# Latent stage: gate arithmetic and gated values on GpSimd, and identity products at other places of TensorE's queue

## The chip, the cores and the metric

The kernel runs on one core of a Trainium2 chip. A core has four compute engines with a queue of instructions each, TensorE (PE in the profile; the loading of its weights is PEld), VectorE (DVE), ScalarE (ACT) and GpSimd (POOL), and SyncE, which here only issues DMAs. Instructions of one engine start in the order in which they are written; between engines, and where a result is read back by the engine that wrote it, they wait on semaphores. Operands lie in SBUF (128 partitions; the profile names two large arenas WK and R) or in the eight PSUM banks ("bank"). The metric is the device time of one execution in microseconds; the kernel is compared by the median of several runs.

## The reference, cut to what matters

A tower of two layers over 32 x 128 tokens of width 192: embedding with a norm, quantised attention, a mixture of attention experts, the "latent" layer (a linear attention with gates, then a gated feed-forward part), and a last layer with attention and routed experts. The change is in the latent layer, of which these lines are computed for each group of tokens:

```
x_norm = rmsnorm(x, ln_w)
latent = silu(x_norm @ w_comp)
q, k, v = split(latent @ w_qkv, 3)
q_f = elu(rope(rmsnorm(q, qn_w))) + 1.0
k_f = elu(rope(rmsnorm(k, kn_w))) + 1.0
params = (latent @ w_reso).reshape(B, L, H, 4)
sem_amp, ctx_amp = sigmoid(params[..., 0]), sigmoid(params[..., 2])
sem_phase, ctx_phase = sigmoid(params[..., 1]) * pi, sigmoid(params[..., 3]) * pi
base_gate = sigmoid(sem_amp * ctx_amp * cos(sem_phase - ctx_phase) * temperature)
gate = clip(base_gate * 1.2 - 0.1, 0.05, 0.95)
kv_input = einsum('blhd,blhe->blhde', k_f, v) * gate[..., None, None]
...                        # decayed running sums over the tokens, times q_f, over their denominator
x = x + rmsnorm(out, memn_w) @ w_proj * silu(latent @ w_outgate)
x = x + silu(rmsnorm(x) @ w1) * (rmsnorm(x) @ w2) @ w3
```

The gate is one number for each token and head: 24 numbers for each partition in a step of the loop. The gated values are v times the gate, 384 numbers for each partition.

## The kernel before, in words

The work runs in stages one after the other: embedding and quantised attention (to about 447 us of the profile), expert attention (to 687), the latent stage (to 1167), the last layer's attention and routing (to 1604, here called the last attention), and the routed experts.

The latent stage treats 4096 tokens as 32 tiles of 128. Two streams of two tiles each (M = 2) take turns, NG = 8 times each, so that there are 16 steps. Each engine has its share of a step written as two generators, `*_l_1` (norm, latent, q, k, v, gates, scores and output) and `*_l_2` (projection, feed-forward part). `in_turns_apart` (L902, its loop L908) writes them out: `alternate(first(g, p1), second(g, p0))`, a piece of one, up to its `yield`, then a piece of the other. So while one stream is in its first half the other is in its second, and on every engine the order of the two is fixed by where the `yield`s stand. Nothing is reordered later.

What the change touches:

- `vector_l_1` (L1526). After the reduction of the squares (L1535) and nine small steps that build inverse roots (L1493 to L1501), VectorE rotates q and k (L1545 to L1549), takes the phase difference `a.z` of the gates (L1552), adds (L1553), scales and clamps each tile (L1556, L1558), forms the amplitude of the gate (L1559, L1560), builds the features (L1565) once ScalarE has the exponentials, forms the argument of the gate's tanh (L1568, L1569), copies half of the turned features out of PSUM (L1573), and multiplies scores by the decay table (L1588, four for each tile). Between the two tiles' L1588 it finishes the gate (L1578, L1579) and multiplies v by it (L1580), after which `f.value` is signalled. L1622 and L1626 belong to the other stream's second half.
- `scalar_l_1` (L1764). ScalarE takes the gates' tanh, silu and a copy of v out of PSUM (L1779 to L1781), then waits for `f.gate_in` and does the sine of `a.z` and its square (L1784, L1786), then the exponentials of the features (L1790, for which it loads another table), copies (L1794), and, when `f.gate_in` has come a second time, the tanh that is the gate (L1798).
- `pool_l_1`, `pool_l_2`. GpSimd only raises variances to the power -1/2 (L1047, called by `roots`).
- `tensor_l_1`, `tensor_l_2`: the product with w_comp (L1007), those with w_cat (L1701, L1704), the turning of the features (L1712), the scores (`products`, L1646), the values (`times_v`, L1656), and of the other stream the turning of the normalised rows (`turn_doubled`, L985 and L987), the hidden layer (L1674, L1682) and the last product (L1741).
- `stirred_f` (L1210) and `stirred` (L2037) are products of the identity with itself into a bank whose content isn't used; the expert attention calls the first, the last attention the second (`tensor_m_1`, L2042).
- The last attention's `tensor_m_1` waits for `f.x` (normalised rows from L1881), turns them, makes its features and scores (L2012), waits for the exponentials of the turned scores (`f.exp`, L2141 on ScalarE) and multiplies by v (L2025).

## Time and profile before

| | |
|---|---|
| median of 3 runs | 1988.45 us (1986.03 to 1989.02) |
| the profiled execution | 1987.9 us, of which the span of the profile is 1986.2 us |
| PE, PEld busy | 1551.4 us (78%), 1187.1 us (60%) |
| DVE busy | 1311.0 us (66%) |
| ACT busy | 959.7 us (48%) |
| POOL busy | 400.6 us (20%) |
| chain that ended last | PE 44%, DVE 37%, ACT 12%, issue 4% |

Busy shares are means over stages with different limits; in the latent stage POOL is busy for 43 of 480 us. The granted clock of TensorE has two levels here, 1.2 and 2.4 GHz, shown as 0.50 and 1.00; a stretch with a number between has parts at either. In a timeline, each row has start and duration in us, engine, line, operation, output and inputs with shapes, and in brackets how long the engine had been idle before it and who released it. A semaphore wait without idle time isn't shown.

### The profile page before, as it was taken

What the parts mean: (1) busy time and instruction counts of PE and PEld (TensorE: products, weight loads), DVE (VectorE), ACT (ScalarE), POOL (GpSimd) and SP (SyncE); (2) the same over time, 40 slices, a digit from 0 to 9 for tenths busy, and PEclk for the clock granted to TensorE, in tenths of its full rate; (3) what the DMA queues carried; (4) which work ended last, traced back from release to release, by engine and by line L of the source; (5) the groups of instructions that cost most, each with busy time, mean ns of one, the idle gap of its engine ahead of it and who ended that gap; (6) DMA issues with size and microseconds to landing.
All of it is one profiled execution on the core that took longest, in us unless ns stands there. A gap on an engine that the chain in (4) does not pass through costs nothing.

```text
span 1986.2 us, 36888 instructions
## 1 busy us (share of the span) xinstructions
PE 1551.4 (78%) x12764; PEld 1187.1 (60%) x12764; DVE 1311.0 (66%) x4361; ACT 959.7 (48%) x2769; POOL 400.6 (20%) x494
## 2 busy tenths in 40 slices
PE   0076764888888667887888868999999949999996
PEld 0032221776666445565555546777777738888885
DVE  7898885787888768878888844666666632222221
ACT  1275999863444544454454423444434324444442
POOL 7401332000000100000000000222222223333332
PEclk9985555569999779989999988999999959999998
DMA  3000000119990000000000000000000027778875
GB/s 75 17 1 1 1 1 1 22 42 185 180 164 5 1 0 1 0 0 0 0 0 0 0 24 3 26 25 24 24 24 24 25 88 181 193 199 192 194 192 141
DMA packets 136264, 113.02 MB, mean 57 GB/s; under 512 B 29417, under 2 KB 128457, under 8 KB 136137
## 3 DMA queue, kind: packets, MB, share of 16 engines
q1 hardware_dynamic: 119320, 91.70, 20.2%
q0 software_dynamic: 16864, 20.33, 5.3%
q8 instruction: 42, 0.69, 0.1%
q14 instruction: 38, 0.30, 0.1%
HBM read 69.19 MB, written 45.94 MB: 58 GB/s over the span
## 4 chain that ended last, share of the span: by engine, by line
PE 44%; DVE 37%; ACT 12%; issue 4%; POOL 1%; DVEq 0%; DMA 0%; ACTq 0%; POOLq 0%; SPq 0%
ACT bank L716 9%; PE bank L2357 8%; PE bank L2347 6%; PE bank L1007 5%; PE bank L2342 3%; PE bank L1000 3%; PE bank L2012 3%; DVE R L1588 2%; DVE WK L1588 2%; DVE R L1864 2%; PE bank L2025 1%; PE bank L2040 1%; PE bank L1712 1%; PE bank L966 1%; PE bank L640 1%
## 5 line engine op out<-in xcount | busy, mean ns | idle before, releaser
L1047 POOL TENSOR_TENSOR WK<-WK,mhalf 128x2 f32<-128x2 f32 (+1 forms) x96 | 78.0, 812 | 806.9 <-DVE WK L1512 324.5
L2394 ACT ACTIVATE R<-bank,R 128x256 f32<-128x256 f32 x234 | 98.2, 471 | 187.3 <-PE bank L2347 185.5
L716 ACT ACTIVATE bank<-bank,nbias,sc 128x128 f32<-128x128 f32 x384 | 168.9, 993 | 21.3 <-POOL nbias L528 21.3
L2274 POOL DMA_INDIRECT moe_sum<-WK x78 | 121.5, 1557 | 229.0 <-DMA moe_sum<-WK 165.3
L2245 DVE SCALAR_TENSOR_TENSOR WK<-bank,R,WK 128x192 f32<-128x192 f32 x78 | 28.9, 413 | 209.4 <-PE bank L2357 209.4
L716 ACT ACTIVATION_READ_ACCUMULATOR bank<-bank,nbias,sc 128x1 f32 x384 | 163.2, 768 | 0.0
L2357 PE MATMUL bank<-R 128*128 128x192 f32 x936 | 158.6, 326 | 0.0
L1007 PE MATMUL bank<-WK,R 96*128 96x256 f32 x576 | 148.3, 400 | 6.5 <-ACT WK L973 3.8
L2357 PEld LDWEIGHTS bank<-R 128*128 128x128 f32 x936 | 151.3, 190 | 0.0
L1007 PEld LDWEIGHTS bank<-WK,R 96*128 96x128 f32 x576 | 106.9, 195 | 26.2 <-ACT WK L973 6.9
L2347 PE MATMUL bank<-R 128*128 128x256 f32 x468 | 112.8, 392 | 0.0
L610 PE MATMUL bank<-R 32*128 32x128 bf16 x384 | 62.9, 300 | 59.9 <-ACT bank L716 57.1
L2347 PEld LDWEIGHTS bank<-R 128*128 128x128 f32 x468 | 86.8, 192 | 23.6 <-issue 13.2
L610 PEld LDWEIGHTS bank<-R 32*128 32x128 bf16 x384 | 29.6, 118 | 118.7 <-ACT bank L716 106.6
L433 DVE TENSOR_REDUCE neg_all<-bank 128x3 f32<-128x384 f32 x128 | 69.5, 554 | 27.3 <-PE bank L610 25.1
L2012 PE MATMUL bank<-WK 32*128 32x128 f32 x1536 | 63.5, 296 | 24.5 <-ACT R L2141 12.4
L559 PE MATMUL bank<-R,wq 96*128 96x512 bf16 x192 | 79.0, 540 | 4.6 <-DVE WK L407 2.7
L1674 PE MATMUL bank<-WK,R 128*128 128x256 f32 x256 | 68.1, 412 | 15.0 <-ACT WK L993 15.0
L1000 PE MATMUL bank<-R,WK 96*128 96x192 f32 x384 | 76.4, 343 | 2.9 <-ACT WK L973 1.4
L528 POOL TENSOR_SCALAR nbias<-neg_all,sc 128x3 f32<-128x3 f32 x128 | 38.6, 301 | 198.1 <-DVE neg_all L433 197.8
L2040 PE MATMUL bank<-ident 128*128 128x128 f32 x480 | 76.6, 299 | 0.0
L315 PE MATMUL bank<-ident,amx 128*1 128x128 f32 (+2 forms) x5 | 1.9, 382 | 93.8 <-DVE amx L351 54.9
(499 smaller groups left out, 3996.9 us busy)
## 6 DMA issues: line engine op xcount, KB each, us to landing
moe_rows_in<-zeros SPq DMA_DIRECT2D x1, 25026.0 KB, 148.2
R<-in_L_ffn_w SPq DMA_DIRECT2D x39, 576.0 KB, 5.0
R<-in_L_ffn_w SPq DMA_DIRECT2D x39, 384.0 KB, 3.1
R<-moe_rows_in SPq DMA_DIRECT2D x39, 194.0 KB, 4.6
R<-in_L_ffn_w SPq DMA_DIRECT2D x78, 96.0 KB, 3.6
R<-in_L_ffn_b SPq DMA_DIRECT2D x39, 96.0 KB, 5.1
moe_sum<-resid POOLq DMA_DIRECT2D x16, 192.0 KB
moe_sum<-WK POOLq DMA_INDIRECT x78, 5.8
```

Source lines behind the costliest of these rows:

```text
L559: mm = nc.tensor.matmul(bank[b][:, :], wq[0:C, c, o * P:(o + 1) * P], tokens(xqT_all, g)[0:C, c, :], start=(c == 0), stop=(c == 1))
L610: mm = nc.tensor.matmul(bank[u % 4][:, k * P:(k + 1) * P], qk[32 * j:32 * j + 32, k, i * P:(i + 1) * P], qk[32 * j:32 * j + 32, 3 + k, i * ...
L716: ins = nc.scalar.activation(s, s, ACT.Exp, bias=nbias[:, u, k:k + 1], scale=col(SS), accum_out=units(sum_all, g, u)[:, k:k + 1])
L1000: mm = nc.tensor.matmul(a.bank[b][:, i * D:(i + 1) * D], a.xT[0:C, c, i * P:(i + 1) * P], w[0:C, c, :], start=(c == 0), stop=(c == 1))
L1007: mm = nc.tensor.matmul(out, w[0:C, c, m], a.xT[0:C, c, :], start=(c == 0), stop=(c == 1))
L1588: nc.vector.tensor_tensor(a.p[:, 4 * i + j, :], a.bank[j][:, 0:384], decay[:, j, :], ALU.mult).then_inc(f.decayed, 1)
L2012: mm = nc.tensor.matmul(a.bank[j][:, k * P:(k + 1) * P], x, y, start=True, stop=True)
L2040: nc.tensor.matmul(a.bank[1][:, 0:P], ident[:, :], ident[:, :], start=True, stop=True)
L2274: pool.indirect_dma_start(out=acc, out_offset=bass.IndirectOffsetOnAxis(ap=x_id[k % B3][:, t:t + 1].bitcast(U32), axis=0), in_=x_y[k % B3] ...
L2347: mm = nc.tensor.matmul(hidden_at(p, n), xw_1a[h][:, q * P:(q + 1) * P], x_T[h][:, 0, :], start=False, stop=True)
L2357: mm = nc.tensor.matmul(bank[7][:, t * D:(t + 1) * D], x_hid[f][:, t * P:(t + 1) * P], xw_2[h][:, f, :], start=(p == 0 and n == 0 and t == ...
L2394: ins = nc.scalar.activation(x_hid[q], hidden_at(p, n), ACT.Gelu, bias=xb_1[h][:, q:q + 1])
```

## The change

Twelve instructions on GpSimd take the place of eight on VectorE (seven on 24 columns and the multiplication L1580), in another form: 1/8 is put into the amplitude, 1 - 2 s^2 is written as amplitude - 2 amplitude s^2, the temperature is applied by ScalarE's tanh (`scale=l_temp`), the constants 0.6 and 0.5 come from a small tile `l_gc` that is filled once, and one instruction on a single column (L1642 of the changed kernel) stands ahead of the clamp. GpSimd waits on a new semaphore `f.gate_w` for its own results. `f.gate_in` now comes three times a step. Two identity products are added ahead of the products with w_cat, five ahead of the turning for the feed-forward part; in the last attention two at the start of `tensor_m_1` go, and the two behind the second tile's turned scores become five ahead of the wait for the first tile's exponentials. Left out of the diff are the counts of semaphores, the two new names in `l_signals` and `take(3)` for `l_gc`.

```diff
...
@@ -1453,7 +1453,8 @@
-            yield
+            for n, x in enumerate((0.6, 0.5, 1.0)):
+                nc.gpsimd.memset(l_gc[:, n:n + 1], x)
             for a in streams:
...
@@ -1462,6 +1463,8 @@
             ins.then_inc(s_pad, 1)
+            pool.wait_ge(s_pad, 4)
+            yield
...
@@ -1548,37 +1551,23 @@
             ch.step(ins)
-            v.wait_ge(f.gates, per(g, 1, 1))
-            nc.vector.tensor_tensor(a.z, a.sg[:, :, :, 1], a.sg[:, :, :, 3], ALU.subtract).then_inc(f.gate_in, 1)
             ch.step(nc.vector.tensor_tensor(a.qk, a.a, a.b, ALU.add))
...
                 nc.vector.tensor_scalar(a.b[:, w], a.a[:, w], 0.0, None, ALU.min).then_inc(f.features_in, 1)
-            ch.step(nc.vector.tensor_scalar(a.pz, a.sg[:, :, :, 2], 1.0, None, ALU.add))
-            ch.step(nc.vector.scalar_tensor_tensor(out=a.amp, in0=a.sg[:, :, :, 0], scalar=1.0, in1=a.pz, op0=ALU.add,
-                                                   op1=ALU.mult))
             for i in range(M):
...
                                                in1=heads(a.qk[:, w]), op0=ALU.max, op1=ALU.add).then_inc(f.pads, 1)
-            v.wait_ge(f.gate_t, per(g, 2, 1))
-            ch.step(nc.vector.tensor_scalar(a.pz, a.z2, -2.0, 1.0, ALU.mult, ALU.add))
-            nc.vector.scalar_tensor_tensor(out=a.pz, in0=a.pz, scalar=l_temp, in1=a.amp, op0=ALU.mult,
-                                           op1=ALU.mult).then_inc(f.gate_in, 1)
             for i in range(M):
...
             decayed(v, g, a, f, 0)
-            v.wait_ge(f.gate_t, per(g, 2, 2))
-            ch.step(nc.vector.tensor_scalar(a.z, a.z, 0.6, 0.5, ALU.mult, ALU.add))
-            ch.step(nc.vector.tensor_scalar(a.z, a.z, 0.05, 0.95, ALU.max, ALU.min))
-            nc.vector.tensor_tensor(a.va[:, :, :, 0:DH], a.r.rearrange("p t (h d) -> p t h d", d=DH),
-                                    a.z.unsqueeze(3).to_broadcast([P, M, H, DH]), ALU.mult).then_inc(f.value, 1)
             decayed(v, g, a, f, 1)
...
@@ -1625,9 +1614,36 @@
+        def of_gate(n):
+
+            return l_gc[:, n:n + 1].to_broadcast([P, M * H]).rearrange("p (t h) -> p t h", t=M)
+
         def pool_l_1(pool, g, a, f):
...
             yield
+            pool.wait_ge(f.gates, per(g, 1, 1))
+            nc.gpsimd.tensor_tensor(a.z, a.sg[:, :, :, 1], a.sg[:, :, :, 3], ALU.subtract).then_inc(f.gate_in, 1)
+            nc.gpsimd.tensor_scalar(a.pz, a.sg[:, :, :, 2], 1.0, None, ALU.add)
+            nc.gpsimd.tensor_scalar(a.amp, a.sg[:, :, :, 0], 0.125, 0.125, ALU.mult, ALU.add).then_inc(f.gate_w, 1)
+            pool.wait_ge(f.gate_w, per(g, 6, 1))
+            nc.gpsimd.tensor_tensor(a.amp, a.amp, a.pz, ALU.mult).then_inc(f.gate_w, 1)
+            pool.wait_ge(f.gate_w, per(g, 6, 2))
+            nc.gpsimd.tensor_tensor(a.pz, a.amp, a.amp, ALU.add).then_inc(f.gate_w, 1)
+            pool.wait_ge(f.gate_w, per(g, 6, 3))
+            pool.wait_ge(f.gate_t, per(g, 2, 1))
+            nc.gpsimd.tensor_tensor(a.pz, a.pz, a.z2, ALU.mult).then_inc(f.gate_w, 1)
+            pool.wait_ge(f.gate_w, per(g, 6, 4))
+            nc.gpsimd.tensor_tensor(a.pz, a.amp, a.pz, ALU.subtract).then_inc(f.gate_in, 1)
+            pool.wait_ge(f.gate_t, per(g, 2, 2))
+            nc.gpsimd.tensor_tensor(a.z, a.z, of_gate(0), ALU.mult).then_inc(f.gate_w, 1)
+            pool.wait_ge(f.gate_w, per(g, 6, 5))
+            nc.gpsimd.tensor_tensor(a.z, a.z, of_gate(1), ALU.add).then_inc(f.gate_w, 1)
+            pool.wait_ge(f.gate_w, per(g, 6, 6))
+            nc.gpsimd.tensor_tensor(a.pz[:, 0, 0:1], l_gc[:, 2:3], l_gc[:, 2:3], ALU.mult)
+            nc.gpsimd.tensor_scalar(a.z, a.z, 0.05, 0.95, ALU.max, ALU.min).then_inc(f.gate_in, 1)
+            pool.wait_ge(f.gate_in, per(g, 3, 3))
+            nc.gpsimd.tensor_tensor(a.va[:, :, :, 0:DH], a.r.rearrange("p t (h d) -> p t h d", d=DH),
+                                    a.z.unsqueeze(3).to_broadcast([P, M, H, DH]), ALU.mult).then_inc(f.value, 1)
...
@@ -1696,6 +1712,7 @@
             product(a, lw_comp, slice(0, LAT), a.bank[1][:, 0:NM]).then_inc(f.lat_p, 1)
+            stirred_f(a, 2)
             pe.wait_ge(f.lat, per(g, 1, 1))
...
@@ -1727,6 +1744,7 @@
             yield
+            stirred_f(a, 5)
             pe.wait_ge(f.ffn_in, per(g, 1, 1))
...
@@ -1780,7 +1798,7 @@
             ins.then_inc(f.gates, 1)
-            act.wait_ge(f.gate_in, per(g, 2, 1))
+            act.wait_ge(f.gate_in, per(g, 3, 1))
             nc.scalar.activation(a.z2, a.z, ACT.Sin, scale=float(np.pi / 4)).then_inc(f.gate_s, 1)
...
@@ -1794,8 +1812,8 @@
             yield
-            act.wait_ge(f.gate_in, per(g, 2, 2))
-            nc.scalar.activation(a.z, a.pz, ACT.Tanh, scale=0.125).then_inc(f.gate_t, 1)
+            act.wait_ge(f.gate_in, per(g, 3, 2))
+            nc.scalar.activation(a.z, a.pz, ACT.Tanh, scale=l_temp).then_inc(f.gate_t, 1)
             for i in range(M):
...
@@ -2040,7 +2058,6 @@
         def tensor_m_1(pe, g, a, f, prev):
-            stirred(a, 2)
             pe.wait_ge(f.x, per(g, 1, 1))
...
@@ -2072,9 +2089,9 @@
             yield
+            stirred(streams[1 - a.n], 5)
             pe.wait_ge(f.exp, per(g, 4 * M, 4))
             scores(pe, g, a, f, 1, f.scoresT, True)
-            stirred(streams[1 - a.n], 2)
             pe.wait_ge(f.exp, per(g, 4 * M, 5))
```

On POOL, at the start of the latent stage, the first root and the fills of the padded tiles were followed by the loop:

```order
L1047 TENSOR_TENSOR WK<-WK,mhalf 128x4
L1458 MEMSET WK 128x1536
L1459 MEMSET R 128x768
L1458 MEMSET R 128x1536
L1459 MEMSET R 128x768
L1463 MEMSET R 128x24 x2
L908 UNCONDITIONAL_BRANCH
L908 ISA
```

Now, behind the last of the same fills and ahead of the loop, the first step's gate stands there with its twelve instructions:

```order
L1625 TENSOR_TENSOR WK<-WK 128x24
L1626 TENSOR_SCALAR WK<-WK 128x24
L1627 TENSOR_SCALAR WK<-WK 128x24
L1629 TENSOR_TENSOR WK<-WK 128x24
L1631 TENSOR_TENSOR WK<-WK 128x24
L1634 TENSOR_TENSOR WK<-WK 128x24
L1636 TENSOR_TENSOR WK<-WK 128x24
L1638 TENSOR_TENSOR WK<-WK 128x24
L1640 TENSOR_TENSOR WK<-WK 128x24
L1642 TENSOR_TENSOR WK<-WK 128x1
L1643 TENSOR_SCALAR WK<-WK 128x24
L1645 TENSOR_TENSOR R<-WK 128x24x16
```

In the loop the same twelve stand behind the other stream's two roots (L1047 128x2) and ahead of the next step's root (L1047 128x4).

On DVE, in the loop, a step from the second part of the rotation (L1549) to the copies out of PSUM was:

```order
L1549 TENSOR_TENSOR R<-R 128x2x192 x2
L1552 TENSOR_TENSOR R<-WK 128x24
L1553 TENSOR_TENSOR R<-R 128x768
L1556 TENSOR_TENSOR R<-R,WK 128x384
L1558 TENSOR_SCALAR R<-R 128x384
L1556 TENSOR_TENSOR R<-R,WK 128x384
L1558 TENSOR_SCALAR R<-R 128x384
L1559 TENSOR_SCALAR R<-WK 128x24
L1560 SCALAR_TENSOR_TENSOR WK<-WK,R 128x24
L1565 SCALAR_TENSOR_TENSOR R<-R 128x24x16 x2
L1568 TENSOR_SCALAR R<-R 128x24
L1569 SCALAR_TENSOR_TENSOR R<-R,WK 128x24
```

The same place in the changed kernel, whose lines are numbered otherwise from here on (L1552 is L1549 of before, L1554 is L1553, L1557 and L1559 are L1556 and L1558, L1563 is L1565):

```order
L1552 TENSOR_TENSOR R<-R 128x2x192 x2
L1554 TENSOR_TENSOR R<-R 128x768
L1557 TENSOR_TENSOR R<-R,WK 128x384
L1559 TENSOR_SCALAR R<-R 128x384
L1557 TENSOR_TENSOR R<-R,WK 128x384
L1559 TENSOR_SCALAR R<-R 128x384
L1563 SCALAR_TENSOR_TENSOR R<-R 128x24x16 x2
L1567 COPY R<-bank 128x384 x2
```

Five small instructions are gone here (L1552, L1559, L1560, L1568, L1569). The other two (L1578, L1579) and the large multiplication L1580 stood between the two groups of four L1588; they now follow each other, as L1577 x8.

On PE, a step of the latent stage from the product with w_comp to the turning for the feed-forward part was, and is now:

```order
L1007 MATMUL bank<-WK,R 128x256 x2
L1701 MATMUL bank<-R 128x384 x2
L1704 MATMUL bank<-R 128x432 x2
L985 MATMUL bank<-ident,WK 128x128
L987 MATMUL bank<-ident,WK 64x128 x2
```

```order
L1007 MATMUL bank<-WK,R 128x256 x2
L1213 MATMUL bank<-ident 128x128 x2
L1718 MATMUL bank<-R 128x384 x2
L1721 MATMUL bank<-R 128x432 x2
L1213 MATMUL bank<-ident 128x128 x5
L985 MATMUL bank<-ident,WK 128x128
L987 MATMUL bank<-ident,WK 64x128 x2
```

Two products (L1213) stand behind L1007 and five ahead of L985. Next, PE in the last attention, from the router's product of one stream to the product with v of the other, before and after:

```order
L2100 MATMUL bank<-R,WK 128x8 x4
L2012 MATMUL bank<-WK 128x128 x12
L2040 MATMUL bank<-ident 128x128 x2
L2025 MATMUL bank<-R 32x128 x12
L2040 MATMUL bank<-ident 128x128 x2
L2044 REGISTER_ALU
L966 MATMUL bank<-ident,WK 96x128 x4
L2025 MATMUL bank<-R 32x128 x12
```

```order
L2117 MATMUL bank<-R,WK 128x8 x4
L2058 MATMUL bank<-ident 128x128 x5
L2030 MATMUL bank<-WK 128x128 x12
L2043 MATMUL bank<-R 32x128 x12
L2061 REGISTER_ALU
L966 MATMUL bank<-ident,WK 96x128 x4
L2043 MATMUL bank<-R 32x128 x12
```

Here L2040 (L2058 in the changed kernel) are the identity products, L2100 (L2117) the router's product, L2012 (L2030) the turned scores, L2025 (L2043) the product with v and L966 the turning of the next rows.

## Rows read from the trace of the kernel before

**Rows 1.** One stretch of the span, the latent stage (start:end, its length, busy us and count of each engine, granted clock, DMA share, GB/s).

```profile
687.00:1167.00 480.00, 372.12 (x3144) 266.54 (x3143) 384.69 (x1192) 230.80 (x638) 42.86 (x54) 0.94 0.00 0
```

**Rows 2.** The same view by steps of the latent stage.

```profile
841.57:873.00 31.43, 26.59 (x184) 18.85 (x180) 23.65 (x74) 14.01 (x40) 2.46 (x3) 0.84 0.00 0
...
902.14:930.23 28.09, 22.31 (x186) 15.84 (x180) 23.63 (x74) 13.93 (x40) 2.46 (x3) 1.00 0.00 0
```

**Rows 3.** The timeline of one step of the latent stage.

```profile
915.33 0.38 ACT L1781 ACTIVATE R<-bank 128x192 f32<-128x192 f32 x1
...
917.35 0.20 DVE L1552 TENSOR_TENSOR R<-WK 128x24 f32<-128x24 f32 x1
...
917.47 0.95 DVE L1553 TENSOR_TENSOR R<-R 128x768 f32<-128x768 f32 x1
...
917.58 0.22 ACT L1784 ACTIVATE R<-R 128x24 f32<-128x24 f32 x1 [1.87 <-DVE R L1552]
...
918.08 1.28 ACT L1790 ACT_TABLE_LOAD   x1
...
919.05 0.36 DVE L1558 TENSOR_SCALAR R<-R 128x384 f32<-128x384 f32 x1
...
920.30 0.52 ACT L1790 ACTIVATE R<-R 128x384 f32<-128x384 f32 x1 [0.34 <-DVE R L1558]
...
923.62 0.95 PE L1646 MATMUL bank<-R 32*128 32x128 f32 x24 [0.85 <-ACT R L1794]
```

**Rows 4.** The same timeline, later in the step.

```profile
927.66 1.95 DVE L1588 TENSOR_TENSOR R<-bank,decay 128x384 f32<-128x384 f32 x4 [0.18 <-PE bank L1646]
...
929.66 1.52 PE L1656 MATMUL bank<-R 128*32 128x128 f32 x48 [0.57 <-DVE R L1588]
```

**Rows 5.** The same timeline, TensorE.

```profile
909.20 1.56 PE L1701 MATMUL bank<-R 128*128 128x384 f32 x4 [0.47 <-ACT R L1768]
...
912.42 0.33 PE L985 MATMUL bank<-ident,WK 128*128 128x128 f32 x1 [0.21 <-DVE WK L1616]
...
914.68 2.00 PE L1674 MATMUL bank<-WK,R 128*128 128x256 f32 x8 [0.94 <-ACT WK L993]
...
921.24 1.53 PE L1712 MATMUL bank<-ident,R 128*128 128x128 f32 x12 [0.70 <-DVE R L1565]
```

**Rows 6.** The timeline where POOL and DVE use SBUF together, two earlier stages.

```profile
38.26 0.19 POOL L2495 TENSOR_TENSOR shift<-less_mean,rs 128x4 f32<-128x4 f32 x1
...
50.43 0.96 DVE L221 SCALAR_TENSOR_TENSOR WK<-resid,pos 128x768 f32<-128x768 f32 x1
...
50.76 0.69 POOL L2495 TENSOR_TENSOR shift<-less_mean,rs 128x4 f32<-128x4 f32 x1
...
203.34 0.99 POOL L523 TENSOR_TENSOR resid<-resid,bprojb 128x384 f32<-128x384 f32 x1
...
203.74 0.88 DVE L422 TENSOR_SCALAR R<-WK 128x512 bf16<-128x512 f32 x1
...
206.38 0.43 DVE L422 TENSOR_SCALAR R<-WK 128x512 bf16<-128x512 f32 x1
```

**Rows 7.** The timeline, five identity products of the expert attention.

```profile
448.30 1.38 PE L1213 MATMUL bank<-ident 128*128 128x128 f32 x10 [1.14 <-DVE amx L1314]
```

**Rows 8.** The stretches view by steps of the last attention.

```profile
1214.06:1242.27 28.21, 25.15 (x270) 21.54 (x270) 12.56 (x40) 11.51 (x27) 1.70 (x2) 0.87 0.01 1
...
1267.91:1291.76 23.85, 21.88 (x249) 18.55 (x248) 16.50 (x65) 9.68 (x25) 6.65 (x8) 1.00 0.08 27
...
1291.76:1316.36 24.60, 22.99 (x262) 19.51 (x266) 16.53 (x66) 10.85 (x27) 6.63 (x8) 1.00 0.08 26
...
1340.22:1366.20 25.98, 24.38 (x251) 20.67 (x252) 16.54 (x66) 10.36 (x25) 6.63 (x8) 0.90 0.07 23
```

**Rows 9.** The timeline in the last attention.

```profile
1318.37 0.64 PE L966 MATMUL bank<-ident,WK 128*96 128x128 f32 x4 [0.72 <-DVE WK L1881]
...
1339.20 0.95 PE L2012 MATMUL bank<-WK 32*128 32x128 f32 x24 [0.71 <-ACT R L2141]
```

8 lines of the change are left out of this document (4 added, 4 removed).

## Prediction

> **What bounds the kernel now.** I read the stretches of the span first, then the latent stage step by step, then the timeline of one step, then the places where POOL and DVE already meet, and last the steps of the last attention. The latent stage takes 480 of 1986 us; DVE is busy for 385 of them, PE for 372, and POOL, which gets the new work, for only 43 [rows 1]. So there is room on POOL, but a mean says nothing about which wait ends last. That is read from one undisturbed step [rows 3 to 5]; the sixteen steps repeat it.
>
> The rows of DVE from the rotation to the clamps carry no idle time in brackets: it works there without a gap, and the phase difference L1552 and the sum L1553 lie in that run [rows 3]. ScalarE waits 1.87 us for L1552, does sine and square, loads a table from 918.08 to 919.36, and has it just before the first clamped tile L1558 is there at 919.41 (start 919.05 and 0.36 of duration). The second exponential starts at 920.30 behind the second L1558 with 0.34 us idle. From there the chain is ScalarE's: exponential, another table, two silus, two copies, and then the scores L1646 at 923.62, which waited for its copy. So DVE is on the path up to 920.3 and not between there and the scores. Between the two groups of four L1588 PE makes the second tile's scores, and DVE waits 0.18 us for them although L1578 to L1580 stand in that place [rows 4]: these three instructions lie in PE's shadow. L1656, which needs the gated values, starts at 929.66, released by the last L1588.
>
> **The change part by part.** The sum is made against the profiled execution's 1987.9 us; the median of the runs shown is 0.55 us above it.
>
> VectorE's work that goes. L1559, L1560, L1568 and L1569 stand behind 920.3, where ScalarE's chain is later, and L1578 to L1580 stand in PE's shadow; I cost them at nothing, and no new wait shows up, because the next things due (ScalarE's copy at 923.62, PE's scores at 927.66) don't depend on them. L1552 is on the path: L1553 starts 0.12 us behind it (917.35 to 917.47), so a step gets 0.12 us shorter. 16 x 0.12 = 1.9 us. Below that no gain, above it none.
>
> GpSimd's chain. The gates' values are there when L1781 ends, 915.71. If a POOL instruction on 24 columns takes 0.2 to 0.7 us, which are the free and the blocked time of one on 4 columns [rows 6], the phase difference is there at 916.0 to 916.5, earlier than DVE's 917.55; even 0.8 us later (the five products, below) it still is in time. ScalarE's wait for it has until 917.58 before the table load becomes late. The last five instructions follow ScalarE's tanh, which stands just behind the copy that released L1646 at 923.62, so at about 924.2: four at 0.2 to 0.7 and a product of 384 columns, 0.99 us for the same shape at L523 [rows 6], give 926.0 to 928.0, and PE needs them at 929.66. Behind the gate in POOL's queue stands the root of the next step, which starts at 930.23 [rows 2], so nothing is late there. Cost 0 in the middle; the far end is a rival.
>
> The Trainium skill, page "GPSIMD Engine Reference", section "4.1 Engine selection", says to keep elementwise work on VectorE since GpSimd is about twice as slow with two inputs. The trace agrees (0.99 us at L523 against 1.95 us for the four L1588, 0.49 us each, all of 384 columns, is its ratio), and by that rule the move would lose; by the row the loss falls into a wait of 1.7 us or more, and the sum doesn't change.
>
> Both engines on SBUF at once. In the changed kernel seven POOL instructions of the gate run beside DVE's unbroken run. Earlier stages show what happens: a POOL product of 0.19 us took 0.69 where DVE's L221, with two inputs in SBUF, was running; L221 itself kept its 0.96. The other way round, L422 on DVE started while POOL's L523 was running and took 0.88 instead of 0.43, to the end of L523 [rows 6]. So whoever comes second waits for the first. A POOL instruction of about 0.2 to 0.3 us that gets in between two of DVE's holds the second for at most its own length. The lower end is 0 a step; the upper end is one collision as long as the one seen, 0.45 a step, 7.2 us. I take 0.1 a step, near the lower end, because the POOL instructions are a fifth as long as L523: 1.6 us.
>
> The Trainium skill, page "SBUF — State Buffer", section "🔬 SBUF: two separate sides", calls it an exclusive lock on a shared pair of ports, taken for a whole instruction, and names DVE's instructions with two SBUF inputs too. The trace agrees for POOL waiting on L221; by that rule each of the seven could stop DVE, and the sum would be worse by up to 16 x 7 x 0.2 = 22 us, an estimate with the 0.19 us of the row.
>
> Three fills of one column each stand in the first step ahead of the large ones, for which DVE and PE wait: bounded by 0 and 3 x 0.19, taken as 0.2 us.
>
> Identity products. Five, shown as ten entries, take 1.38 us [rows 7], so two about 0.55. The two behind L1007 fall into a wait of 0.47 us and PE has its silu'd input at 909.20 [rows 5]: with the overlap of successive products they just fit, 0 to 0.1 us. The five stand ahead of L985, where PE waited only 0.21 us [rows 5]. L985 gets about 0.8 us later, with it the hidden layer (L1674 waits 0.94 for ScalarE's copy, and that wait moves along), which ended at or before 920.5 and now ends by about 921.3; the turning L1712 waited 0.70 us there. So nearly all of it is absorbed, and what is left is behind ScalarE's table anyway. In the last attention, L966 waits 0.72 us behind the two products that go, and the five that come stand in a wait of 0.71 us and delay the second turned scores by about 0.4 to 0.6 us [rows 9]; L966, behind them, waits for DVE and not for them. I cost the direct time of all at 0.
>
> What they can give back is the clock. An undisturbed step of the latent stage takes 28.09 us at a granted clock of 1.00; the step at 841.57 took 31.43 with 0.84 [rows 2], 3.3 us more. Of ten such rows two others are below 1.00 behind the stage's cold start and add 0.8. In the last attention steps alternate between 24.60 and 23.85 us. The step from 1214.06 took 28.21 with 0.87 and the one from 1340.22 took 25.98 with 0.90, 4.4 and 1.4 us more [rows 8]; of fourteen such rows five others lie below 1.00 and add 4.6. Together 4.1 + 10.4 = 14.5 us are lost to stretches in which half the clock, 1.2 GHz, was granted. The drops follow PE's light stretches: in the latent stage the small turnings L985 with waits on either side, in the last attention the router's product and the wait at 1339.20. The five products stand just there. But in the latent stage the light stretch behind them (L985 to L1674) stays as long as it was, and two products elsewhere go. Ends: all 14.5 us back, or two more drops like 31.43's, 6.6 us lost. I take a third back: 4.9 us.
>
> Sum: 1987.9 - 1.9 + 1.6 + 0.2 - 4.9 = 1982.9 us profiled, 1983.5 as a median.
>
> **Rivals.**
>
> The clock isn't helped. The drops come at other steps, as many as before. Then 1987.8 profiled, 1988.3 us. For it: the latent stage has undisturbed steps with exactly the same gaps as the disturbed one, so the gaps alone don't decide. Against: the products fill the emptiest place.
>
> The drops all go: 1987.8 - 14.5, so 1973.8 us. For it: the expert attention already has such products in its waits [rows 7], and its steps show few drops. Against: the long wait ahead of L966 and L1000 is left as it is.
>
> POOL's first subtraction comes late (slower). If it misses its gap between the L1549 and waits for L1553 (0.95 us from 917.47, so to 918.42), the phase difference ends at about 918.7, the sine starts 1.15 us later than 917.58, and table, exponentials and all of ScalarE's chain follow, because the table load had 0.05 us to spare. 16 x 1.15 = 18.4 us instead of the 1.6: 1999.7 profiled, 2000.2 us. It decides from a phase difference later than 917.6 on. For it: L2495 waited out a whole L221. Against: the gates are there at 915.71 and the phase difference is wanted at 917.58, with two seams between DVE's instructions before that.
>
> PE becomes late. If the five products delay the hidden layer by more than L1712's wait of 0.70 us, by up to 0.5 a step, 8 us come on top, 1987.8 + 8 - 4.9 and so 1991.4 us. For it: 1.38 less 0.21 is more than 0.70. Against: successive products overlap, and ScalarE's table load hides some.
>
> **How the numbers follow.** A measurement of this kernel tells 0.2%, 4.0 us, from no change. My forecast (clock partly helped) has 37%, the clock not helped 25%, all drops gone 15%, POOL late 12%, PE late 11%. Faster by over 0.2%, under 1984.5: 30 of the 37, all of the 15, 2 of the 25, 0.47. Slower, over 1992.4: all 12, 5 of the 11, 3 of the 25, 0.20. The rest 0.33. The range reaches down past the case without drops, 1973.8, to 1972 (no cost of the shared SBUF at all), and up past PE's late case, a third of the way to POOL's late chain, to 1995; the longer way to 2000 is left out.
>
> **What would show it.** Right: L1784 starts before 917.6 in the same step's time and the first exponential still waits for DVE; the undisturbed steps take 28.0 and 29.0 us; POOL's product ends more than 1 us ahead of L1656; fewer steps below a clock of 1.00. Wrong: the exponential's table load ends behind L1558, L1553 and L1558 on DVE are longer than 0.95 and 0.36 us, L1712 has no wait left, or as many steps below 1.00 as before.

## The result: faster by 18 us, more than forecast, and the profile after

The changed kernel takes 1970.09 us in the median of five runs (1966.6 to 1974.8) against 1988.64 us (1986.03 to 1989.07); the ratio is 0.991, interval 0.9894 to 0.9925. The forecast was 1983.5 with a range from 1972 to 1995, so the direction was right and the time lies 2 us below the range. The profiled execution took 1969.73 us, its span is 1968.1 us. Two executions of this study ran in a slower state and stand in no time or ratio given here: one of the kernel before, of 4086.57 us, beside e8 to e11, and one of e13, of 2076.66 us.

Split at the same instructions of both traces, the spans differ like this:

| stretch | before | after | difference |
|---|---|---|---|
| up to the first step of the latent stage | 687.19 | 685.94 | -1.25 |
| fifteen steps of the latent stage | 444.10 | 436.87 | -7.23 |
| its last half step, opening of the last attention | 58.14 | 59.26 | +1.12 |
| fifteen steps of the last attention | 374.14 | 364.44 | -9.70 |
| the rest | 422.62 | 421.59 | -1.03 |

The two loops hold nearly all of it. The first row lies ahead of anything that was changed (over all traces of this study the latent stage begins between 683.3 and 689.5 us). The stretches view of the kernel after, the latent stage and two of its steps, then three steps of the last attention (columns as in rows 1):

```profile
687.00:1167.00 480.00, 389.10 (x3380) 296.12 (x3381) 364.18 (x1063) 233.41 (x643) 124.37 (x249) 0.95 0.00 0
838.58:866.60 28.02, 23.41 (x198) 17.70 (x194) 22.30 (x66) 14.01 (x40) 7.62 (x15) 1.00 0.00 0
866.60:895.50 28.90, 24.67 (x246) 18.95 (x242) 22.44 (x67) 14.55 (x40) 7.59 (x15) 1.00 0.00 0
1206.87:1232.02 25.15, 23.20 (x274) 19.89 (x276) 12.56 (x40) 11.41 (x27) 1.71 (x2) 1.00 0.01 1
1328.55:1353.14 24.59, 22.54 (x268) 19.16 (x260) 16.52 (x67) 10.41 (x25) 6.65 (x8) 1.00 0.07 24
1353.14:1376.98 23.84, 21.80 (x248) 18.81 (x252) 16.48 (x65) 9.79 (x24) 6.64 (x8) 1.00 0.07 25
```

Here every step behind the first of each loop is at a granted clock of 1.00, but for the second of the latent stage (0.94), which still holds the end of the cold start. The two first steps have 0.55 and 0.78, as before the change (0.55 and 0.77). Against [rows 8] the steps of the last attention are as long as the undisturbed ones of before (24.60 and 23.85), so nothing was gained there but the drops: 28.21 became 25.15, and 25.98 became 24.59. In the latent stage two things came together: no drop, and shorter steps, 28.02 against 28.09 us [rows 2], and 28.90 against 29.15 for the long ones.

The timeline of one step of the latent stage after the change:

```profile
908.72 1.99 PE L1690 MATMUL bank<-WK,R 128*128 128x256 f32 x8 [0.94 <-ACT WK L993]
...
909.83 0.45 POOL L1625 TENSOR_TENSOR R<-WK 128x24 f32<-128x24 f32 x1 [5.30 <-ACT R L1799]
...
910.31 0.22 ACT L1802 ACTIVATE R<-R 128x24 f32<-128x24 f32 x1 [0.56 <-POOL R L1625]
...
910.72 0.96 DVE L1554 TENSOR_TENSOR R<-R 128x768 f32<-128x768 f32 x1
...
910.82 0.95 POOL L1627 TENSOR_SCALAR WK<-WK 128x24 f32<-128x24 f32 x1
...
912.70 0.52 ACT L1808 ACTIVATE R<-R 128x384 f32<-128x384 f32 x1 [0.62 <-DVE R L1559]
...
913.48 1.23 DVE L1563 SCALAR_TENSOR_TENSOR R<-R 128x384 f32<-128x384 f32 x2
...
913.59 0.52 ACT L1808 ACTIVATE R<-R 128x384 f32<-128x384 f32 x1 [0.37 <-DVE R L1559]
...
914.40 1.47 PE L1729 MATMUL bank<-ident,R 128*128 128x128 f32 x12
...
915.26 1.21 DVE L1567 COPY R<-bank 128x384 f32<-128x384 f32 x2 [0.55 <-PE bank L1729]
...
918.93 0.84 POOL L1645 TENSOR_TENSOR R<-R 128x384 f32<-128x384 f32 x1
...
920.95 1.95 DVE L1577 TENSOR_TENSOR R<-bank,decay 128x384 f32<-128x384 f32 x4 [1.07 <-PE bank L1662]
```

POOL's phase difference is there at 910.28, 0.44 us before VectorE even begins the sum L1554; the rival of a late POOL chain did not come. ScalarE has its table 0.62 us ahead of the first clamped tile, where it had 0.05 us to spare before [rows 3], so VectorE's run alone sets when the exponentials start. The gated values end at 919.77, 3.2 us ahead of the product that needs them. The turning L1729 has no wait left (0.70 before, [rows 5]): the five products took up just the room that was read there. The prediction had named this as a sign of being wrong, and it came; what it was to show, longer steps, didn't. VectorE's copies behind it now wait for it, some 0.55 us, but ScalarE, which has the table load to do, doesn't, and the step got no longer. And POOL does collide with VectorE, but it is POOL that pays: L1627, on 24 columns, takes 0.95 us, as long as the L1554 that it stands beside. L1554 itself takes 0.96 against 0.95 before [rows 3].

### The profile page after: what moved, and what is told of

Read it like the earlier page. It is cut to its first block, busy times and chain, and to the rows that moved or that the text cites. A ratio compares the mean times of both kernels' runs of the same rounds, so it can differ in the third digit from the quotient of the medians.

```text
span 1968.1 us, 37567 instructions
## 1 busy us (share of the span) xinstructions
PE 1551.7 (79%) x13020; PEld 1205.5 (61%) x13020; DVE 1289.9 (66%) x4233; ACT 961.6 (49%) x2769; POOL 481.7 (24%) x689
## 4 chain that ended last, share of the span: by engine, by line
PE 46%; DVE 34%; ACT 12%; issue 4%; POOL 2%; DVEq 0%; DMA 0%; ACTq 0%; POOLq 0%; SPq 0%
ACT bank L716 9%; PE bank L2374 8%; PE bank L2364 6%; PE bank L1007 5%; PE bank L2359 3%; PE bank L1000 3%; PE bank L2030 2%; PE bank L1690 2%; DVE R L1577 2%; DVE WK L1577 2%; DVE R L1882 2%; PE bank L966 1%; PE bank L640 1%; PE bank L641 1%; PE bank L1718 1%
## 5 line engine op out<-in xcount | busy, mean ns | idle before, releaser
L1047 POOL TENSOR_TENSOR WK<-WK,mhalf 128x2 f32<-128x2 f32 (+1 forms) x96 | 78.7, 819 | 546.0 <-DVE WK L1024 247.1
L1007 PE MATMUL bank<-WK,R 96*128 96x256 f32 x576 | 147.5, 398 | 6.2 <-ACT WK L973 3.5
L1007 PEld LDWEIGHTS bank<-WK,R 96*128 96x128 f32 x576 | 106.2, 194 | 25.9 <-ACT WK L973 6.6
L2140 ACT ACTIVATE WK<-bank,R 128x256 f32<-128x256 f32 x96 | 40.3, 471 | 69.4 <-PE bank L1007 69.4
L966 PE MATMUL bank<-ident,WK 128*96 128x128 f32 x320 | 53.0, 290 | 26.1 <-DVE WK L1899 11.6
```

The source lines that it names most:

```text
L1007: mm = nc.tensor.matmul(out, w[0:C, c, m], a.xT[0:C, c, :], start=(c == 0), stop=(c == 1))
L1047: nc.gpsimd.tensor_tensor(a.rs[:, 0:n], a.ve[:, 0:n], mhalf[:, 0:n], ALU.pow).then_inc(f.root, 1)
```

## Experiments

The kernel before, run many times beside these, gave anything from 1977.8 to 1992.1 us in one set; the fastest of these runs had a mean granted clock of 0.887, the slowest 0.877. So the same program loses more or less to low-clock stretches from run to run. A "drop" is such a stretch inside a step. The verdicts below rest on medians, and on steps of the traces, which don't depend on how many drops a run had.

### One part of the change at a time

e1 puts the identity products back (only the gate is changed). The other three leave the gate on VectorE: e2 has only the products of the latent stage, e3 only those of the last attention, e4 both. Edits against the kernel before, cut at "...":

```diff
 e2, e4:    product(a, lw_comp, ...).then_inc(f.lat_p, 1)
+           stirred_f(a, 2)
 ...
 e2, e4:    yield
+           stirred_f(a, 5)
            pe.wait_ge(f.ffn_in, per(g, 1, 1))
 ...
 e3, e4: def tensor_m_1(pe, g, a, f, prev):
-           stirred(a, 2)
 ...
 e3, e4:    yield
+           stirred(streams[1 - a.n], 5)
            pe.wait_ge(f.exp, per(g, 4 * M, 4))
            scores(pe, g, a, f, 1, f.scoresT, True)
-           stirred(streams[1 - a.n], 2)
```

> The change with the identity products put back where they were in both stages: only the gate on GpSimd is left. Theory (products keep the clock up, the gate is worth little): the undisturbed steps of the latent stage become 0.06 us (short ones) to 0.25 us (long ones) shorter, some 2.5 us in all, the steps of lower clock stay, as many as before in both stages (14.5 us), and the median is 1986 us (1984 to 1989). Rival 1 (the gate's move brought much of the gain, because VectorE's chain is shorter): under 1980. Rival 2 (where drops fall is a matter of how the steps happen to lie in time, and any edit moves them): the drops are at other steps, and their sum may be anything between 0 and 14.5 us.

> The kernel before with the two and the five identity products of the latent stage, nothing else. Theory (each stage's products keep that stage's clock): no step of the latent stage below a clock of 1.00 behind the cold start, the last attention as before (25.6 to 28.2 us at its disturbed steps), a gain of 4 us and so 1984.5 us (1982 to 1987). Rival 1 (gate): no gain, 1988.6, or a loss of up to 5 us, since the five products delay the hidden layer by 0.7 us while DVE isn't relieved. Rival 2 (alignment): the drops move in both stages, and the last attention changes too although nothing of it is changed.

> The kernel before with the changed products of the last attention only (two at the start of its step gone, two moved and made five). Theory: no step of the last attention below 1.00 but its cold start, the latent stage as before; about 10 us gained, 1978.5 us (1976 to 1982). Rival 1 (gate): no gain. Rival 2 (alignment): part of the drops stay, at other steps, 1980 to 1988.

> All identity products as in the change, the gate still on VectorE. Theory: no drops in both stages, 14.5 us gained, 1974 us (1971 to 1977), so that the changed kernel's 1970.1 is this and some 3 to 4 us of the gate. Rival 1 (gate): above 1980. Rival 2 (alignment): drops left in one of the stages.

| | median, us | ratio to before, interval | undisturbed latent steps | latent steps with a drop | low-clock stretches in the last attention |
|---|---|---|---|---|---|
| e1 gate | 1987.53 | 0.9997 (0.9983 to 1.0011) | 28.10, 28.98 | 4 | 8 |
| e2 latent products | 1987.46 | 0.9999 (0.9985 to 1.0013) | 28.07, 29.14 | 2 | 6 |
| e3 last attention | 1981.62 | 0.9973 (0.9958 to 0.9988) | 28.08, 29.14 | 6 | 0 |
| e4 e2 and e3 | 1976.39 | 0.9949 (0.9929 to 0.9969) | 28.07, 29.15 | 3 | 0 |

Before had 3 such latent steps and 8 such stretches. The last attention is settled: with its products moved, not one drop; without, 6 and 8. The gate and the latent products alone are worth nothing in the median, where some 2.5 and 4 us were expected: their traces still have drops, e1 even a step of 31.36 us, and e2's two contradict its expectation of none. e3 and e4 lie in their ranges, but above the times named, and e4 has three drops where none was expected. Compared with each other, e4 is 5.2 us below e3: on top of the last attention's products those of the latent stage are worth something, with the gate still on VectorE. The undisturbed steps say who shortened them: the products hardly (28.07, 29.14), the gate by 0.17 us in the long ones. The stretches of e3's last attention, at the place of a drop before:

```profile
1337.76:1362.35 24.59, 22.56 (x268) 19.19 (x260) 16.53 (x66) 10.38 (x25) 6.63 (x8) 1.00 0.07 24
1362.35:1386.19 23.84, 21.79 (x247) 18.80 (x250) 16.48 (x65) 9.80 (x24) 6.62 (x8) 1.00 0.07 25
```

### The changed kernel again, and with one part out

e5 is the changed kernel once more; e6 leaves out the two and the five products of the latent stage, e7 the two only. Edits against the changed kernel, cut at "...":

```diff
 e6, e7
-            stirred_f(a, 2)
             pe.wait_ge(f.lat, per(g, 1, 1))
 ...
 e6
-            stirred_f(a, 5)
             pe.wait_ge(f.ffn_in, per(g, 1, 1))
```

> The changed kernel, nothing left out, once more. What is open: whether the latent stage is free of drops because products and gate together remove their cause, or by chance in the one profile, as the steps happened to lie in time. Theory (cause removed): again every step behind the stage's first two at 1.00, 28.0 and 28.9 us, and 1970 us (1966 to 1975). Rival (chance): one to four steps of the latent stage below 1.00, each 0.6 to 3.3 us longer, and a median nearer to 1975.

> The changed kernel without the two and five products of the latent stage: gate on GpSimd, and the changed products of the last attention. The last attention is free of drops in any theory. Theory (the latent products are needed too): four or so steps of the latent stage below 1.00, as where the gate alone was moved, 8 us, and 1979 us (1976 to 1984). Rival (the gate's shorter steps do it, the latent products are worth nothing, as they were by themselves): no more drops than in the changed kernel and the same time within 2 us, 1970 to 1972.

> The changed kernel without the two products behind L1007, the five ahead of L985 kept. Theory (the five do it, since the light stretch begins at L985): like the changed kernel, 1970 us (1966 to 1975), no drops in the latent stage. Rival (the two count as much, since each wait that is filled counts): one to three steps below 1.00 and 1973 to 1978.

e5 took 1971.45 us (1966.93 to 1976.82, ratio 0.9931, 0.9911 to 0.9951), and one of its latent steps has a drop (29.70 us). So "no drop" in the first profile was partly luck. e6 took 1977.76 (0.9953, 0.9937 to 0.9969), with two drops: added to gate and last attention, the latent products are worth some 6 us, much as without the gate (e4 against e3), though alone they showed nothing. The intervals of these neighbours overlap, so the 5 to 6 us are rough. They also shorten the undisturbed steps once the gate is on POOL: e6 has 28.10 and 28.97, like e1, against 28.02 and 28.90; the five do this, since e7 has 28.03 and 28.90. e7 took 1972.77 us in the median (0.9952, 0.9916 to 0.9987), but its runs fall into two groups: seven from 1967.1 to 1975.3 us and three from 1992.8 to 1994.6, above every run of the changed kernel (at most 1976.8 in twelve). So the two are not idle either, against its expectation. The profiled run is one of the three, 1992.8 us, and the most telling trace of all: five short steps at a clock of 0.84 to 0.89, four of them the same. The stretches view of e7, one such step and its three parts:

```profile
901.07:933.60 32.53, 27.70 (x198) 20.11 (x191) 22.13 (x65) 14.16 (x40) 6.55 (x15) 0.84 0.00 0
901.07:905.24 4.17, 2.65 (x30) 1.51 (x19) 3.21 (x15) 2.31 (x9) 1.62 (x2) 1.00 0.00 0
905.24:915.48 10.24, 9.74 (x20) 6.48 (x21) 4.89 (x15) 3.60 (x12) 0.87 (x2) 0.50 0.00 0
```

And the kernel before, its slow step of [rows 2] and the start of that of [rows 8], cut in the same way:

```profile
841.57:845.77 4.20, 2.65 (x27) 1.51 (x19) 3.21 (x15) 2.33 (x9) 1.67 (x2) 1.00 0.00 0
845.77:856.01 10.24, 9.77 (x20) 6.40 (x21) 4.98 (x16) 3.52 (x11) 0.79 (x2) 0.50 0.00 0
856.01:873.00 16.99, 14.18 (x139) 10.93 (x141) 15.46 (x44) 8.16 (x21) 0.00 (x0) 1.00 0.00 0
1340.22:1340.70 0.48, 0.48 (x4) 0.38 (x4) 0.16 (x1) 0.48 (x2) 0.23 (x1) 1.00 0.00 0
1340.70:1344.12 3.42, 3.42 (x33) 2.62 (x32) 1.81 (x5) 1.75 (x6) 0.77 (x1) 0.50 0.00 0
```

The clock falls 4.2 us into the step in both, ahead of the five products and even of the two (6.4 us in). It falls behind a stretch in which PE worked 2.65 of 4.2 us. Over all traces of latent stages up to here, each drop of a short step begins 3.5 to 4.9 us into it. So the latent products stand behind the place where this clock is lost. The two stand inside the drop, though, and there they seem to matter: in all traces of this study no drop of a short step lasts over 6.9 us in a kernel that has them (ten drops), and without them eight of nineteen last 10.2 or 10.3 us. That is a count and no tested cause.

Two of before's three drops are of another kind. They begin 13.5 us into a long step, and there the prediction had the place right. The stretches view of before and its timeline:

```profile
811.82:825.30 13.48, 10.57 (x83) 6.69 (x76) 9.61 (x38) 7.48 (x25) 2.46 (x3) 1.00 0.00 0
825.30:828.71 3.41, 3.41 (x11) 2.32 (x11) 3.25 (x9) 1.40 (x6) 0.00 (x0) 0.50 0.00 0
...
824.73 3.27 PE L1674 MATMUL bank<-WK,R 128*128 128x256 f32 x8 [0.94 <-ACT WK L993]
```

This fall comes 0.6 us behind the end of the light stretch from L985 to L1674, ahead of which the five now stand. None of the kernels with the five has a drop of this kind (e2 and e4 with the gate on VectorE among them), and none with the gate on POOL and without the five has one either (e1, e6 and, below, e10). In before both together cost 1.2 us, against 3.3 us for the one in the short step.

In the last attention the drop of before begins at 1340.70, 1.5 us behind the end of the wait of 0.71 us of [rows 9], and the five moved products stand exactly in that wait. From this came the next set.

### Place against number

Four products in the wait of 1.33 us that ends 2.8 us into a step, behind the turning back: e8 adds them to the changed kernel, e9 has only them and the last attention's change, e10 has them in place of the two and five. e11 takes the last attention's numbers but leaves the place of before. e8 and e10 are edits of the changed kernel, e9 and e11 of the kernel before:

```diff
 e8, e9, e10
             turned_back(pe, g, a, f, 1)
+            for _ in range(4):
+                nc.tensor.matmul(a.bank[1][:, 0:P], ident[:, :], ident[:, :], start=True, stop=True)
             pe.wait_ge(f.out, per(g, M, M))
 ...
 e11
         def tensor_m_1(pe, g, a, f, prev):
-            stirred(a, 2)
 ...
             scores(pe, g, a, f, 1, f.scoresT, True)
-            stirred(streams[1 - a.n], 2)
+            stirred(streams[1 - a.n], 5)
```

> The changed kernel with four more identity products in each latent step, behind the turning back (L1680) and ahead of the wait for the output's rows (L966). In all profiles so far the latent stage's low-clock stretches begin 3.5 to 4.9 us behind the start of a short step, so ahead of the two and the five products of the change, and right behind this wait of 1.33 us. Theory (a drop is prevented by products ahead of where it begins, those behind only shorten it): no drop in the latent stage, and 1969 us (1965 to 1973), a little under the changed kernel's 1970 to 1971. Rival (place doesn't matter, only how many): also none, so this run tells nothing of the two by itself. Rival (four products delay L966): each step 0.1 to 0.3 us longer, 1973.

> The kernel before with the last attention's changed products and, in the latent stage, only the four ahead of L966: no two, no five, gate on VectorE. Theory (the place decides): no drops at 3.5 to 4.9 us into a step, undisturbed steps of 28.1 and 29.15 us, and 1973 us (1970 to 1976), better than 1976.4 with the two and five in their places. Rival (the gate's move is what makes the drops rarer): two to five drops left, 1978 to 1983.

> The changed kernel with the four ahead of L966 in place of the two and the five of the latent stage. Theory (place): no drops that begin 3.5 to 4.9 us into a step, 1970 us (1967 to 1974). Rival (the two and five are needed, since they end a drop early and shorten the long steps by 0.1 us): 1975 to 1979.

> The kernel before with the last attention's products changed in number but not in place: the two at the step's start gone, and five instead of two behind the second tile's turned scores (as written before the change), none ahead of them. The latent stage as before. Theory (place): the drops of the last attention stay, three to five pairs of 1.4 to 2 us, and 1986 us (1982 to 1990). Rival (number): no drops there, as with the change's place, and 1981 us.

e11 took 1988.54 us (0.9999, 0.9986 to 1.0013) and kept its drops in the last attention; a pair of its steps, by the stretches view:

```profile
1344.62:1370.71 26.09, 24.49 (x253) 20.78 (x254) 16.53 (x66) 10.28 (x25) 6.64 (x8) 0.90 0.07 23
1370.71:1395.36 24.65, 23.05 (x253) 19.91 (x254) 16.48 (x65) 10.10 (x24) 6.64 (x8) 0.96 0.07 24
```

Where the five stand, by the timelines of the changed kernel and of e11:

```profile
1326.68 1.36 PE L2058 MATMUL bank<-ident 128*128 128x128 f32 x10
1327.97 0.95 PE L2030 MATMUL bank<-WK 32*128 32x128 f32 x24
...
1343.63 0.95 PE L2012 MATMUL bank<-WK 32*128 32x128 f32 x24 [0.71 <-ACT R L2140]
1344.51 1.92 PE L2040 MATMUL bank<-ident 128*128 128x128 f32 x10
```

In e11 they come some 1.7 us later, counted from the router's product, the wait of 0.71 us ahead of L2012 stays empty, and they do nothing: there the place decides. Its trace has eight drops in this stage, as before's has.

In the latent stage e8 took 1970.37 us (0.9906, 0.9881 to 0.9932), e9 1974.45 (0.9931, 0.9904 to 0.9958), e10 1972.02 (0.9918, 0.9892 to 0.9945), with four runs each, all as expected, like e11's. None of their traces has a drop at 3.5 to 4.9 us of a short step. The pairs that differ by the four alone show the gain: e9 lies 7.2 us below e3, and their intervals only touch, at 0.9958; e10 lies 5.7 us below e6, with overlapping intervals. e9, in which the gate stays on VectorE and the five are absent, has two drops of the other kind: 13.5 us into one long step and 13.6 us into the last full one. This kind stands in before, e3, e9 and e11 alone, the kernels that have neither the gate on POOL nor the five ahead of L985. That is read from sixteen traces and is not a tested cause. The price of the four is nothing, by the wait in the changed kernel and by e8's timeline:

```profile
898.32 0.64 PE L966 MATMUL bank<-ident,R 128*96 128x128 f32 x4 [1.33 <-DVE R L1588]
...
900.42 1.06 PE L1741 MATMUL bank<-ident 128*128 128x128 f32 x8
901.91 0.64 PE L966 MATMUL bank<-ident,R 128*96 128x128 f32 x4 [0.43 <-DVE R L1588]
```

Of the 1.33 us of waiting 0.43 are left, and e8's undisturbed steps are 28.01 and 28.89 us. In the medians, though, e8 isn't below the changed kernel.

### What of the gate shortens the steps, and the starts of stages

e12 puts the phase difference back on VectorE, e13 the gated values, both against the changed kernel. In e12 the addition of 1 on POOL (`a.pz`) also became an instruction with two inputs. e14 is e8 with products once at the starts and ends of stages. Cut at "...":

```diff
 e12
-            nc.gpsimd.tensor_tensor(a.z, a.sg[:, :, :, 1], a.sg[:, :, :, 3], ALU.subtract).then_inc(f.gate_in, 1)
+            v.wait_ge(f.gates, per(g, 1, 1))
+            nc.vector.tensor_tensor(a.z, a.sg[:, :, :, 1], a.sg[:, :, :, 3], ALU.subtract).then_inc(f.gate_in, 1)
             ch.step(nc.vector.tensor_tensor(a.qk, a.a, a.b, ALU.add))
 ...
-            nc.gpsimd.tensor_scalar(a.pz, a.sg[:, :, :, 2], 1.0, None, ALU.add)
+            nc.gpsimd.tensor_tensor(a.pz, a.sg[:, :, :, 2], of_gate(2), ALU.add)
 e13
             decayed(v, g, a, f, 0)
+            v.wait_ge(f.gate_in, per(g, 3, 3))
+            nc.vector.tensor_tensor(a.va[:, :, :, 0:DH], ..., ALU.mult).then_inc(f.value, 1)
             decayed(v, g, a, f, 1)
 ...
-            pool.wait_ge(f.gate_in, per(g, 3, 3))
-            nc.gpsimd.tensor_tensor(a.va[:, :, :, 0:DH], ..., ALU.mult).then_inc(f.value, 1)
 e14 (against e8)
 tensor_l_1:
+            if isinstance(g, int) and g == 0:
+                stirred_f(a, 13)
 ...
             pe.wait_ge(f.gates, per(g, 1, 1))
+            if isinstance(g, int) and g == 0:
+                stirred_f(a, 16)
 ...
 tensor_l_2:
-            stirred_f(a, 5)
+            stirred_f(a, 14 if isinstance(g, int) and a.n else 5)
 ...
 tensor_m_1:
+            if not prev and not a.n:
+                stirred(streams[1 - a.n], 10)
```

> The changed kernel with the phase difference back on VectorE, behind the rotation, the rest of the gate on GpSimd. Theory (the gate's gain per step is this one instruction leaving VectorE's unbroken run): undisturbed steps become 0.12 us longer than 28.02 and 28.90, so 28.14 and 29.02 us, 2 us in all, lost in the spread of the medians (1970 to 1976). Rival (the gain of the long steps, 0.25 us, is from somewhere else, or the shared SBUF costs something that goes away with it): steps unchanged within 0.03 us, or shorter.

> The changed kernel with the gated values multiplied on VectorE between the two tiles' decay products, as before the change; the gate itself stays on GpSimd. Theory (that instruction stood in TensorE's shadow): undisturbed steps as in the changed kernel, 28.02 and 28.90 us within 0.03, and the wait of DVE for the second tile's scores falls from 1.07 us to about 0.5. Rival (it was on the path, or its POOL form costs DVE time): steps 0.2 us or more longer or shorter.

> The changed kernel with the four products ahead of L966 and, once each, products in the long waits where stages begin and end at the low clock: 13 ahead of the first rows of the latent stage (a wait of 6.33 us), 16 ahead of the first turning of features (8.05 us), 14 in place of 5 in the stage's last step (2.86 us), 10 ahead of the first rows of the last attention (4.93 us). Theory (products ahead of a stretch bring the clock up for it): the first latent step falls from 35.6 to some 33 us, the one behind it from 31.2 to 30 us, the step that opens the last attention from 25.1 to 24 us, and the time to 1965 us (1960 to 1969). Rival (a single burst in a wait doesn't hold the clock until the work arrives): 1970 us as with the four alone.

The stretches view, a long and a short undisturbed step of e12, then of e13:

```profile
812.64:841.80 29.16, 24.67 (x246) 18.88 (x238) 22.57 (x68) 14.57 (x40) 6.96 (x14) 1.00 0.00 0
841.80:869.96 28.16, 23.42 (x202) 17.70 (x198) 22.41 (x67) 13.99 (x40) 7.37 (x14) 1.00 0.00 0
```

```profile
810.29:839.18 28.89, 24.66 (x248) 18.94 (x238) 22.89 (x68) 14.59 (x40) 6.76 (x14) 1.00 0.00 0
839.18:867.20 28.02, 23.41 (x202) 17.70 (x196) 22.77 (x67) 13.97 (x40) 6.78 (x14) 1.00 0.00 0
```

One instruction of 0.20 us, the phase difference, is worth 0.13 us of a short step and 0.26 of a long one, so all that the gate gave. e12's steps are 0.02 to 0.08 us longer than those of e2, which has the same products and the whole gate on VectorE; that is what the rest of the gate on POOL costs, in e12's form. e13's steps are those of the changed kernel; its wait for the second tile's scores is 0.61 us against 1.07, so the values product was indeed hidden. e13 took 1973.82 us (0.9922, 0.9897 to 0.9947), with two drops in the latent stage. e12's median, 1981.09 (0.9961, 0.9944 to 0.9979), is 10 us above the changed kernel's and outside the 1970 to 1976 us expected; the longer steps explain 3 us of it (fifteen by 0.2). Two latent steps of its trace have a drop of 2.9 us each, and its runs' mean clock is 0.889 against 0.892, so it has more low clock; why, I can't say.

In a long step of e12 the timeline shows where the 0.26 comes from:

```profile
942.83 0.20 DVE L1555 TENSOR_TENSOR WK<-WK 128x24 f32<-128x24 f32 x1
942.95 1.00 DVE L1556 TENSOR_TENSOR WK<-WK 128x768 f32<-128x768 f32 x1
...
945.87 0.52 ACT L1809 ACTIVATE WK<-WK 128x384 f32<-128x384 f32 x1 [0.38 <-DVE WK L1561]
```

The sum L1556 starts 15.67 us into the step; in e13, without the small instruction, its twin starts at 15.45. So it cost 0.22, not the 0.12 between its start and the next one's, since the instruction behind it starts sooner after the pair of L1552 than the small one did. The remaining 0.04 us is the length of the sum itself (1.00 against 0.96).

e14 took 1965.68 us (0.9887, 0.9859 to 0.9916; 1961.3 to 1967.3), below both kernels: none of its four runs comes up to the changed kernel's median, though the interval of its ratio overlaps with that one's (0.9894 to 0.9925). By the stretches view, its first two latent steps and the step that opens the last attention:

```profile
684.70:717.78 33.08, 21.66 (x144) 17.50 (x148) 25.41 (x72) 14.71 (x37) 8.84 (x23) 0.76 0.00 1
717.78:749.53 31.75, 27.77 (x242) 22.08 (x238) 22.39 (x65) 15.54 (x41) 7.63 (x15) 0.91 0.00 1
1176.74:1199.02 22.28, 18.00 (x157) 15.59 (x157) 10.95 (x24) 5.03 (x10) 3.91 (x7) 0.91 0.11 33
```

Against e8, 35.7 became 33.1 and 25.1 became 22.3 us at higher clocks; 33 and 24 were expected. The second latent step didn't fall (31.75 against 31.2), against the expectation: the clock fell again at the end of the first.

## Why the prediction was wrong

**The clock term** was the step that failed: "I take a third back: 4.9 us". Between the two profiles all came back: the drops of both loops, counted against undisturbed steps, were worth 4.5 us in the latent stage and 9.8 in the last attention, 14.3 together. That is close to the 14.5 of the prediction, by errors that partly cancel: the step of 28.21 us was priced at 4.4 us against a step of another kind, and undisturbed it takes 25.15, so it lost 3.1. This size stood in the text as a rival with 15%, 1973.8 us; with the 2.2 us of the shorter steps it comes near what was measured. The last 1.7 us lie between the profiles with no cause shown. That the first profile had no drop at all in the latent stage was luck in part (e5 has one), and in medians the last attention's products alone gave 5 us (e3), not 9.8, with six drops in the latent stage of that trace. The third was a choice between two ends, not a reading. The rows would have told more: the drop of 1340.70 begins behind a wait, and the diff puts five products into that very wait. In the last attention the term should have been near the whole: e3, e4 and every later kernel with the moved products show no drop there.

**The placement in the latent stage** was misread for the costly drop: "The five products stand just there". The light stretch from L985 to L1674 is the place of the two drops in long steps, 1.2 us; the one of 3.3 us falls 4.2 us into a short step, ahead of all products, behind the wait for L966 that the prediction itself named as left as it is. That the products help anyway, by 5 to 6 us (e4 against e3, the changed kernel against e6), and that there isn't always a clean stage (e5), is shown; how they help from behind isn't. In the traces with two and five, a drop of a short step adds 1.4 to 2.9 us, with neither 1.3 to 3.3, with the five alone up to 4.5. The condition I named against the rival "clock isn't helped" (the products fill the emptiest place) was wrong for the short steps.

**L1552 off the path** was right as a mechanism and small in size: 0.12 a step forecast, 0.13 and 0.26 measured by e12. **The shared SBUF** was forecast at 0.1 a step, and e12 against e2 gives 0.02 to 0.08; the direction of the wait was half wrong, since it is mostly POOL's L1627 that waits out L1554. Together the undisturbed steps gained 0.07 and 0.25 us, some 2.2 us where the sum had nearly zero.

**POOL's price.** The runs show it: 0.84 us for the values on POOL, 0.55 on VectorE in e13, 1.5 times as long, and it doesn't matter where a wait of over 1 us hides it. The rule of the Trainium skill, page "GPSIMD Engine Reference", section "4.1 Engine selection", to keep elementwise work on VectorE, would have forecast a loss, which didn't come. The exclusive lock of the Trainium skill, page "SBUF — State Buffer", section "🔬 SBUF: two separate sides", is seen in this case's trace (0.95 us at L1627), but not the 22 us that VectorE would have lost by it.

**Hidden work** was read rightly where it was tested: the multiplication L1580 cost nothing on VectorE (e13), the five products are absorbed by the waits behind them (e2: undisturbed steps unchanged), POOL was in time. The other six small instructions were not put back one by one; that e12's one instruction accounts for all that the steps gained fits their cost of nothing.

**What stays open:** why the latent products and the gate show nothing alone, but each some 4 to 7 us beside the last attention's products (e4 and e6 against e3, the changed kernel against both), why e12 has more low clock than its steps explain, why the steps with five products gained 0.08 us once the gate was on POOL, and what sets which of equal steps is struck.

## What to carry to other kernels

Where a trace shows steps of equal work and unequal length, cut the long one at the clock's changes first: products that only keep TensorE busy removed every drop where they stood in the wait just ahead of the fall. Some 1.7 us later in the queue they removed none in the last attention (e11), and behind the fall in the latent stage they only helped in part. Read what such drops cost as a whole, and give the case that all of it comes back the chance that their place deserves. An instruction in an unbroken run of the critical engine can cost more than the distance to the next start: here 0.13 to 0.26 us a step for one of 0.20 us. And look at all runs and not at the median alone: with two small products fewer (e7) the median stayed, but three runs of ten were 20 us longer.

## What the runs showed of the hardware

The same kernel spread over 14 us from run to run, and its fastest run had the higher mean granted clock (0.887 against 0.877). TensorE's clock fell to 0.50 although no wait of the engine in the 4.2 us ahead of it was longer than 1.34 us (before, the step from 841.57). POOL instructions on 24 columns took 0.23 to 0.30 us late in the step (L1638, L1643) and one of them 0.95 us beside a VectorE sum with two inputs in SBUF (L1627).
